# One adapter pair instead of eight masked adapters in a fused four-layer fp32 kernel

## The reference

```python
x = x + (einsum(x, W0[id0[b]]) + b0[id0[b]])             # L0: one of 16 experts
x = x + (einsum('btd,od->bto', x, W1)                    # L1: shared weight, and
         + (x @ A[ad[b]].T) @ Bm[ad[b]].T * scalings[ad[b]])  #  one of 8 adapters of rank 16
x = x + attention(x)     # L2: q, k, v; RMS norm; rotary; paged cache, window of 256; Wo
x = x + (einsum('bct,bcd->bdt', x, W3[id3[b]]) + b3[id3[b]])
```

## Time and profile before

| | |
|---|---|
| median of 3 runs | 998.45 us (997.99 to 999.91) |
| the profiled execution | 999.21 us, of it 997.4 us span from first to last instruction |
| PE busy | 941.9 us (94% of the span) |
| DVE, ACT, POOL busy | 602.1, 386.0, 512.9 us |
| granted TensorE clock | 0.991 of full speed |
| phase one / phase two | about 0 to 516 us / 516 to 997 us |

### The profile page before, as it was taken

One profiled execution on the slowest core, in us unless ns is written; L12 is line 12 of the kernel. 1 busy time (PEld: TensorE's weight loads), 2 busy tenths in 40 slices (PEclk: granted clock), 3 DMA queues, 4 the chain that ended last, 5 costly groups with the idle time before them and its releaser, 6 DMA issues.

```text
span 997.4 us, 22018 instructions
## 1 busy us (share of the span) xinstructions
PE 941.9 (94%) x6253; PEld 683.0 (68%) x6253; DVE 602.1 (60%) x1788; ACT 386.0 (39%) x1061; POOL 512.9 (51%) x469
## 2 busy tenths in 40 slices
PE   5899999999999999999977999999899999999997
PEld 4566766766766766766755777777677777777775
DVE  5434434656656644356455667776676777677775
ACT  2122122221221221221225556565565656565653
POOL 1245555455455477564565455555455555555530
PEclk9999999999999999999999999999999999999999
DMA  9879877767777667778355565566466565566641
GB/s 299 271 260 315 294 277 265 261 217 271 247 229 274 235 235 260 239 245 281 133 171 172 155 194 165 182 188 184 142 186 190 161 211 192 167 181 191 201 137 44
DMA packets 96458, 212.48 MB, mean 213 GB/s; under 512 B 29051, under 2 KB 35160, under 8 KB 88226
## 3 DMA queue, kind: packets, MB, share of 16 engines
q1 hardware_dynamic: 66434, 145.53, 43.7%
q0 software_dynamic: 25088, 57.74, 19.8%
q10 hardware_dynamic: 4896, 8.73, 2.4%
HBM read 204.39 MB, written 33.86 MB: 239 GB/s over the span
## 4 chain that ended last, share of the span: by engine, by line
PE 91%; DVE 2%; issue 2%; DMA 2%; ACT 1%; another core or an unknown queue 1%; SPq 1%; POOL 0%; ACTq 0%; DVEq 0%; POOLq 0%
PE banks L589 11%; PE banks L755 10%; PE banks L803 10%; PE banks L707 9%; PE banks L791 6%; PE banks L628 6%; PE banks L636 6%; PE banks L638 6%; PE banks L778 5%; PE banks L732 3%; PE banks L839 3%; PE banks L697 3%; PE banks L712 3%; PE banks L796 2%; PE banks L599 2%
## 5 line engine op out<-in xcount | busy, mean ns | idle before, releaser
L548 POOL DMA_INDIRECT ring<-new_rows,idx x128 | 130.8, 1022 | 85.0 <-DVE big L1280 33.9
L460 POOL TENSOR_TENSOR rms<-ss,neg_half 128x12 f32<-128x12 f32 x31 | 70.8, 2284 | 182.0 <-DVE ss L1185 181.0
L931 ACT ACTIVATE big<-big,neg_max 128x320 f32<-128x320 f32 x256 | 141.6, 555 | 5.1 <-DVE neg_max L1243 3.8
L1243 DVE CUSTOM_DVE_ANT_0 big<-banks,mask 128x320 f32<-128x320 f32 x256 | 114.6, 486 | 17.7 <-PE banks L755 13.1
L755 PE MATMUL banks<-kt,q_in 64*128 64x192 f32 (+2 forms) x768 | 103.7, 366 | 20.9 <-remote 12.3
L589 PE MATMUL banks<-ring 128*64 128x512 f32 x512 | 117.1, 599 | 3.0 <-DMA ring<-in_w 3.0
L872 ACT ACTIVATE x2t_hi<-banks 128x512 fp32r<-128x512 f32 x32 | 19.1, 597 | 235.7 <-PE banks L599 235.7
L755 PEld LDWEIGHTS banks<-kt,q_in 64*128 64x128 f32 x768 | 79.0, 188 | 44.5 <-remote 16.9
L501 POOL DMA_INDIRECT ring<-in_kvrows,idx x64 | 61.1, 955 | 63.3 <-PE banks L755 45.8
L537 POOL DMA_INDIRECT ring<-new_rows,idx x64 | 61.4, 960 | 57.7 <-PE banks L778 36.2
L589 PEld LDWEIGHTS banks<-ring 128*64 128x64 f32 x512 | 33.9, 136 | 81.4 <-issue 80.3
(11 more groups left out here) (169 smaller groups left out, 2015.3 us busy)
## 6 DMA issues: line engine op xcount, KB each, us to landing
ring<-in_w SPq DMA_DIRECT2D x62, 1024.0 KB, 6.4
ring<-in_xt SPq DMA_DIRECT2D x32, 256.0 KB
x_in<-in_x SPq DMA_DIRECT2D x32, 256.0 KB, 5.5
bias_in<-in_b SPq DMA_DIRECT2D x64, 128.0 KB, 5.5
x_dram<-x SPq DMA_DIRECT2D x32, 256.0 KB, 5.1
q_dram<-q_t ACTq DMA_DIRECT2D x32, 256.0 KB
new_rows<-kv_out SPq DMA_DIRECT2D x32, 256.0 KB, 5.0
q_in<-q_dram SPq DMA_DIRECT2D x32, 256.0 KB
```

Of the source, the lines that this page charges most:

```text
L548: pool.indirect_dma_start(out=kv[:, s, c, :], out_offset=None, in_=new_rows, in_offset=bass.IndirectOffsetOnAxis(ap=idx[:, b, 1 + c:2 + c] ...
L931: nc.scalar.activation(prob[:, s % 2, PLACE[g] * NK:(PLACE[g] + 1) * NK], sm[:, s % 2, g, :], ACT.Exp, bias=neg_max[:, s % 2, g:g + 1], sc ...
L1243: V.tensor_tensor_reduce(sm[:, s % 2, g, :], ps_s[g], mask[:, s % 2, k0:k0 + NK], 1.0, 3.0e38, ALU.add, ALU.min, accum_out=neg_max[:, s % ...
```

## The change

There are three edits. None of them touches phase two.

1. **Each pair's two adapters alone.** For every pair, ACT reads the two adapter numbers with a register load, issues two DMAs that bring the own B of each sequence (16 rows, three copies below one another, 48 rows) into `pair_b`, and copies the 16 columns of A, times the scaling, three times side by side into `pair_a` (`take_adapters`). The A product is now two 64x64 tiles per chunk, one for each sequence (`adapt_down`). The three copies are the three roles of the split product: rows 0 to 15 hold low·, rows 16 to 31 and 32 to 47 the hi/lo combinations. ACT rounds with a 0/1 scale per row (`xa_hi`, `pair_b_hi`), and DVE subtracts (`xa_parts`, `pair_b_parts`), so that one matmul of type fp32r with 128 stacked rows gives what the plain fp32 product gave.
2. **Query transposes behind Q/K/V.** On PE `transpose_queries` follows `project_inputs`; on ACT the copy and the store of the queries come last in the step.
3. **POOL's position factors** are made ahead of `sum_x_bias`.

Besides, `adapt_down` stands between the low parts of Q and of K/V from step 2 on, and `lora_b`, `lora_mask` and their loads go.

```diff
+            def adapt_down(k, s):            # PE
+                pe.wait_ge(pa_ready, k + 1)
+                pe.wait_ge(x1t_ready, k + 1)
+                wait(pe, xa_ready, k)
...
+                for c in range(DC):
+                    for h in range(2):
+                        last = nc.tensor.matmul(ps_la[T * h:T * h + T, 0:T], pair_a[:, s, h, c, :], x1t[:, c, T * h:T * h + T], ...)
+                last.then_inc(la_done, 1)
...
                     for ps_out, n0 in ((ps_q, 0), (ps_kv, D)):
+                        if n0 == D and on(k, 0, NP) and not (isinstance(k, int) and k == 1):
+                            adapt_down(k, s)
...
-                if on(k, 2, NP) and not (isinstance(k, int) and k == NP):
-                    transpose_queries(k, s)
...
-                    project_inputs(k)
+                    project_inputs(k, s)
+                if on(k, 2, NP):
+                    transpose_queries(k, s)
...
-                    for c in range(DC):
-                        last = nc.tensor.matmul(ps_la[:, 0:P], lora_a[:, c, :], x1t[:, c, :], start=(c == 0), stop=(c == DC - 1))
...
-                    nc.tensor.matmul(ps_l1[:, :], xam[:, s, :], lora_b[:, :], start=False, stop=True).then_inc(h_done, 1)
+                    pe.wait_ge(xa_ready, k + 1)
+                    pe.wait_ge(pb_ready, k + 1)
+                    nc.tensor.matmul(ps_l1[:, :], xa_parts[:, :], pair_b_parts[:, s, :], start=False, stop=True).then_inc(h_done, 1)
...
+            def take_adapters(k, s):         # ACT
+                for h in range(2):
+                    n = act.value_load(ids_sb[0:1, 3, bass.ds(k * 2 + h, 1)], min_val=0, max_val=NA - 1)
+                    act.dma_start(pair_b[T * h:T * h + ROLE_ROWS, s, :], a["lb"][bass.ds(n, 1)]...).then_inc(ld_pb[s], 16)
+                    last = nc.scalar.activation(pair_a[:, s, h, :, 0:ROLE_ROWS]..., lora_a[:, :, bass.ds(n * RANK, RANK)]..., ACT.Copy,
+                        scale=scaling[:, bass.ds(n, 1)])
+                last.then_inc(pa_ready, 1)
+            def round_adapters(k, j, s):     # ACT
+                act.wait_ge(ld_pb[s], 2 * 16 * (j + 1))
+                wait(act, pb_ready, k)
+                nc.scalar.activation(pair_b_hi[:, :], pair_b[:, s, :], ACT.Copy, scale=fcols[:, BPART:BPART + 1]).then_inc(pb_hi_ready, 1)
...
+            act.wait_ge(ld_la, 16)
+            for k in range(2):
+                take_adapters(k, k)
+            round_adapters(0, 0, 0)
...
+            def split_adapters(k, s):        # DVE
+                dve.wait_ge(pb_hi_ready, k + 1)
+                wait(dve, h_done, k - 1)
+                V.tensor_tensor(pair_b_parts[:, s, :], pair_b[:, s, :], pair_b_hi[:, :].bitcast(F32), ALU.subtract).then_inc(pb_ready, 1)
...
+            split_adapters(0, 0)
             loop(dve, phase_one, 2, 4, NP + 2, PREP_STEP)
```

More of the change, by code:

```diff
@@ L34 @@
 EPS = 1e-6
+ROLES = 3
+XPART, BPART = 1, 7
+ROLE_ROWS = ROLES * RANK
 NONE = 60000
@@ L485, in phase_one @@
                                             cs[:, s, :].unsqueeze(1).to_broadcast([P, 2, P]), ALU.mult).then_inc(tab_ready, 1)
+                if on(k, -1, NP) and not (isinstance(k, int) and k == 1):
+                    sum_x_bias(k + 1, j + s, 1 - s)
                 if isinstance(k, int) and k in SIDE:
@@ L600, in transpose_x2, with project_inputs @@
                 last.then_inc(t2_done, 1)
-            def project_inputs(k):
+            def adapt_down(k, s):
+                pe.wait_ge(pa_ready, k + 1)
+                pe.wait_ge(x1t_ready, k + 1)
+                wait(pe, xa_ready, k)
+                if isinstance(k, int) and k == NP - 1:
+                    pe.wait_ge(idx_ready, 1)
+                for c in range(DC):
+                    for h in range(2):
+                        last = nc.tensor.matmul(ps_la[T * h:T * h + T, 0:T], pair_a[:, s, h, c, :], x1t[:, c, T * h:T * h + T],
+                                                start=(c == 0), stop=(c == DC - 1))
+                last.then_inc(la_done, 1)
+            def project_inputs(k, s):
                 if isinstance(k, int) and k == NP:
@@ L886, in phase_one @@
                     nc.scalar.activation(wqkv_hi[:, :, D:], wqkv_stage[:, :, D:], ACT.Copy).then_inc(w_hi_ready, 1)
-                if on(k, 2, NP) and not (isinstance(k, int) and k == NP):
-                    store_queries(k, s)
                 if isinstance(k, int) and k == NP:
@@ L908, in phase_one @@
                     nc.scalar.activation(kv_out[:, r, 256:512], ps_kv[:, 256:512], ACT.Copy).then_inc(sqv_ready, 1)
-            loop(act, phase_one, 2, 4, NP + 1, NP)
+                if on(k, 2, NP) and not (isinstance(k, int) and k == NP):
+                    copy_queries(k, j, s)
+                    store_queries(k, s)
+                if on(k, -2, NP):
+                    take_adapters(k + 2, s)
+            loop(act, phase_one, 2, 4, NP + 1, NP - 2)
             act.wait_ge(ld_wo, 16)
@@ L1169, in phase_one @@
                 if on(k, 0, NP):
-                    dve.wait_ge(la_done, k + 1)
-                    wait(dve, h_done, k - 1)
-                    V.tensor_tensor(xam[:, s, :].rearrange("p (h t) -> p h t", h=2), ps_la[:, 0:P].rearrange("p (h t) -> p h t", h=2),
-                                    lora_mask[:, bass.ds(k * 2, 2)].unsqueeze(2).to_broadcast([P, 2, T]), ALU.mult).then_inc(xam_ready, 1)
+                    dve.wait_ge(xa_hi_ready, k + 1)
+                    wait(dve, h_done, k)
+                    for h in range(2):
+                        t0, t1 = T * h, T * h + T
+                        last = V.tensor_tensor(xa_parts[t0:t1, t0:t1], ps_la[t0:t1, 0:T], xa_hi[t0:t1, :].bitcast(F32), ALU.subtract)
+                    last.then_inc(xa_ready, 1)
+                if on(k, -1, NP):
+                    split_adapters(k + 1, r)
                 if isinstance(k, int) and k == 0:
```

81 lines of the change are left out of this document (45 added, 36 removed).

## The result

| | before | after |
|---|---|---|
| median of the runs | 999.18 us (997.99 to 1002.53) | 1010.48 us (1007.93 to 1013.71) |
| the profiled execution's span | 997.4 us | 1009.5 us |
| experts of step 1 begin | 36.03 | 50.58 (+14.55) |
| experts of step 3 begin | 63.67 | 80.58 (+16.91) |
| a steady step, mean of 28 | 15.12 | 14.92 |

The ratio is 1.0118, 95% interval [1.0094, 1.0142]: slower by 11.3 us, where I had forecast 1001.1 us and a range of 994 to 1010. The starts of the experts' groups on PE's timeline place the loss: 14.55 us at the start, 2.36 in steps 1 and 2, 5.47 won back in the 28 steps from 3 to 31, 0.45 lost behind step 31, and 0.2 in phase two: +12.1 of span. These terms come from one trace of each kernel.

A forecast was written before the change was run, and what follows sets the result against it. PE, busy 100 of 100 us in phase one, was taken to bound the kernel. Terms +9.5 + 0.4 - 0.7 - 7.3 + 0.8 = +2.7 us from the median 998.45 gave 1001.1 us, 8-in-10 range 994 to 1010.

The forecast's parts named there:

- The start: +9.5 and +0.4.: Program start: first x1 waits for B's load, L1 starts 9.5 us later; ACT's pair 2 groups in step 1 add 0.4.
- The bound of +13.5 at the landing's end: Upper bound of the start's loss: B landing after 9.3 us and register loads waiting for the engine, +13.5 us.
- Step 1 has no query transposes: -0.7: Step 1: B and A products get shorter, no moved query transposes add time, so it saves 0.7 us.
- Steps 2 to 30 are 29: -7.3.: The 29 steady steps of phase one, each 0.25 us shorter on PE, together save 7.3 us.
- A steady step: -0.25 us.: PE's steady step: B product -0.62, A product -0.06, query transposes +0.43, together -0.25 us.
- that case: A product at 62 ns a matmul under firmware decode: 1.21 us, 0.46 a step more, 1014 us; at most 3 in 100.
- The old place becomes idle.: Steady step on PE: query transposes' old place stays empty, projections still start at 4.93, the new place adds 0.43 us.
- DVE, ACT and POOL in the step.: Steady step: x2 about 1 us late but hidden, ACT done about 1.5 us into the next, position factors give nothing.
- The last step: +0.8.: Behind step 31 nothing covers x2, so DVE's lateness counts and the steady gain is missing: +0.8 us.
- the place didn't close: Rival: query transposes' old place closes up, a step gains 0.43 us more, to 988.6 us; 0.18 together with partial cases.
- the small tiles weren't slow: Rival, chance 0.14: A product's records take 0.056 us each, a step grows 0.12 us, to 1012 us.
- ACT was late: Rival, chance 0.07: ACT's groups take 3 us, PE waits at the projections, for example 0.5 us a step, to 1016.

The follow-up runs named there:

- the repeat: Changed kernel with 65 instead of 6 dummy matmuls behind the first experts and 20 transposes behind pair 0's B product, run again: 1008.08 us, ratio 1.0082.
- the second trace of the changed kernel: The changed kernel run once more, unedited, on another chip beside the repeat: 1011.25 us, ratio 1.0115.
- first run with dummies: Changed kernel with 65 instead of 6 dummy matmuls behind the first experts and 20 transposes behind pair 0's B product: ratio 1.0122.

## Why the prediction was wrong

The direction was right, and so was the wait behind the main loss; the size wasn't, and 1010.48 us lies 0.5 above the range. Two steps of the working failed: it put TensorE's slower clock behind the new wait at nothing, and it priced steps 1 and 2 by PE alone, without POOL's sum for pair 2. The forecast was +2.7 of span, the trace has +12.1. The 9.4 us between them, term by term:

- **"The start: +9.5 and +0.4."** It is +14.55, 4.65 more. x1 ends at 30.30 for 29.3 (issue at 21.16 for 20.9, landing 7.0 for 6.4): 1.0. The larger part is PE's clock, a term the sum doesn't have. I counted when L1's inputs are ready and shifted all behind it by 9.5 as it stood, with projections at the full clock, though a wait of 12 us was what I forecast. That the clock costs something there could be read off: L707's first four matmuls take 2.04 us, and 1.17 in a steady step. The projections after the wait cost 2.81. The rest, about 0.8, I put down to the slowed dummies and A product, behind which xa_hi, the second rounding and wq's rounding hang: L1 begins 11.8 us late, not 9.5; that it now runs at the full clock gives nothing back, since x2 comes directly behind DVE's split of wq (37.69 to 39.98), as foreseen. The bound of +13.5 at the landing's end didn't cover it either. The runs with dummy matmuls show the clock as cause of the 2.81: 9.82 falls to 7.04, and 9.83 to 7.00 in the repeat.
- **"Step 1 has no query transposes: -0.7", "Steps 2 to 30 are 29: -7.3."** Steps 1 and 2 were treated as if nothing but PE could bind there. They cost +2.36 where I had -0.95: 3.3 us (1.8 in the second trace of the changed kernel). Step 1 did get shorter (-2.31), step 2 longer (+4.67). What was overlooked: pair 2's sum has a place of its own behind the rotation, written in the code and visible in the trace as a sum that ends 0.1 us before its reader. I looked at x1 in a steady step and in step 1, and not in step 2. Moving the sum took the wait out, and with it 3.6 to 5.1 us. How long the wait is hangs in part on the clock that step 1 got: 3.62 us with a step 1 of 10.26, 2.04 with one of 11.84.
- **"A steady step: -0.25 us."** It is -0.20 by its terms: B product -0.63 (predicted -0.62), query transposes +0.35 (+0.43), A product with its two changes of shape 0.62 + 0.24 = 0.86 for 0.81, so +0.05 (-0.06), and 0.03 in L1. The record takes 39 ns, between my 0.033 and 0.056, and the changes of shape 0.24 in all, for 0.22. Over 28 steps -5.47 for -7.0: 1.5 us. The changes of shape cost what they were taken to cost. The Trainium skill (TensorE: Matmul & The Clock Gate, the section on 56 against 53.3 ns) gives some 62 ns a matmul with hardware decode off. The 39 ns a record here, and the 48 ns in the forecast, don't speak against it as I took them to: two records are one matmul of the program, so the A product takes 78 ns a matmul. No run here shows whether that case holds; the A product cost 0.62 us and not the 0.99 without switches that the forecast drew from it.
- **"The old place becomes idle."** Right, alone and inside the change. But that the edit is a loss inside the change was wrong: there it saves 0.8 us a step. It didn't enter the sum.
- **"DVE, ACT and POOL in the step."** x2's addition comes at 305.31, 1.05 behind the B product's end, and is hidden, as said. ACT's two groups are later than said: the second copy ends at 306.90, 2.6 us into the step for 1.5, and 1.7 us are left to x2t_hi. No wait in 27 of 28 steps. The position factors give nothing.
- **"The last step: +0.8."** 0.45. Phase two, for which I had nothing, has 0.2.

The range was too narrow because its bounds came from the landing and the record alone; it had no case in which PE's own durations change, nor one for the steps that are written apart. Of the rivals, none happened: the place didn't close, the small tiles weren't slow, ACT was late in one step by 0.2 us. The errors didn't cancel: all three large ones, 4.65, 3.3 and 1.5, went the same way, and only the last step (0.35) went the other.

## What to carry to other kernels

A wait added at a kernel's start can cost more than its length, if it leaves TensorE idle: price the work behind it at the lower clock too, here 3.8 us for 2.1 in the first eight projections, and see which work ran at the lower clock before and no longer does, here L1. Steps at the start of a loop that are written apart have their own order on the slow engines; look there for operands that end just before their reader, since such a wait is invisible until something moves. And price an edit against its absence in the changed kernel, not only against the kernel before: the same move cost 0.48 us a step alone and saved 0.8 in company. Last, take two traces of a kernel before a term of 1 or 2 us at its start is believed.

## What the runs showed of the hardware

- In a wait of 13.5 us without a matmul the granted clock was 0.54 (20 to 30 us), and it was still 0.55 over the next five us, 4.64 of them busy, then 1.00; after a further 2.7 us of idle it was 0.63 and 0.69 over ten us. With PE kept busy by dummy matmuls through the same waits (first run with dummies) the windows from 20 to 60 us all show 1.00, and the one from 65 to 70, behind step 2's wait of 3.65 us, 0.66.
- The same kernel's step 1 took 10.26 us in one trace and 11.84 in another, by the clock at its L1.
- 16 records (8 matmuls of the program) of 128x64 tiles with 64 columns moving take 0.62 us, 39 ns a record; two changes of shape in the midst of fp32r work cost 0.24 us.
- The 96 KB loads of B land after 2.2 to 8.7 us, median 4.6. The one that set the start took 7.0, with the DMA share at 1.07 from 20 to 30 us.
- ACT spends 1.2 us from group to group (register load, DMA, copy) at the start and 1.8 to 2.0 in the loop (303.96 to 305.95, 318.90 to 320.70), where a register load of 0.27 us was the median on SP's queue.
